# TensorE's order within a slot: the second maxima tile goes between the two transposed products of the second head

## The reference

```python
x = x + _L0_attn_a_ref(_layernorm(x, axis=-1), ...)   # causal mask
x = x + _L0_ffn_ref(_layernorm(x, axis=-1), ...)      # tokens split into two classes
x = x + _L0_attn_b_ref(_layernorm(x, axis=-1), ...)   # rotary, no mask
x = x + _L0_ffn_ref(_layernorm(x, axis=-1), ...)      # classes again
```

## Time and profile before

| | us |
|---|---|
| median of 3 runs (lowest, highest) | 5199.68 (5198.17, 5214.73) |
| the profiled execution | 5192.83 |
| its span, first to last instruction | 5191.0 |
| PE busy, DVE busy, ACT busy in the span | 4514.9, 3178.9, 2550.6 |
| CAUSAL stage, 0 to 1485 us: PE busy, DVE busy | 1234.4, 716.5 |
| first SPLIT stage, 1485 to 2830 us | 1176.6, 883.1 |
| ROTARY stage, 2830 to 4125 us | 1143.8, 810.1 |
| last SPLIT stage, 4125 to 5191 us | 960.1, 769.2 |

### The profile page before, as it was taken

The page is one execution under the profiler, slowest core; times in us unless marked ns, Lnnn a source line. Parts: engine busy times, 40 slices in busy tenths (PEclk is TensorE's granted clock), DMA queues, the critical chain, the costliest instruction groups (busy, mean ns, idle before and its releaser), DMA issues. The chain is left out here.

```text
span 5191.0 us, 90278 instructions
## 1 busy us (share of the span) xinstructions
PE 4514.9 (87%) x26116; PEld 1909.3 (37%) x26116; DVE 3178.9 (61%) x6578; ACT 2550.6 (49%) x3362; POOL 1655.2 (32%) x922
## 2 busy tenths in 40 slices
PE   4988988899869999899995999999989599889889
PEld 2444444445413333333332333333333233333333
DVE  3545545455447667676663766666666277777776
ACT  1444444444435554455551655555555265555555
POOL 2354544545422434434434133332333300000000
PEclk8999999999979999999997999999999799999999
DMA  4343434344223334233232223323323322222221
GB/s 148 97 149 125 143 119 145 123 135 135 94 67 104 95 92 120 81 110 107 94 109 81 83 87 116 114 87 104 114 89 103 83 75 84 80 79 80 75 75 51
DMA packets 302300, 525.68 MB, mean 101 GB/s; under 512 B 58340, under 2 KB 236136, under 8 KB 285544
## 3 DMA queue, kind: packets, MB, share of 16 engines
q1 hardware_dynamic: 259432, 485.06, 31.5%
q10 hardware_dynamic: 42496, 35.66, 2.1%
HBM read 316.97 MB, written 201.46 MB: 100 GB/s over the span
## 5 line engine op out<-in xcount | busy, mean ns | idle before, releaser
L923 DVE TENSOR_REDUCE neg_max<-scores 128x1 f32<-128x512 f32 (+3 forms) x4096 | 2490.0, 636 | 1448.8 <-PE scores L1282 856.2
L1141 ACT ACTIVATE probs<-scores_t 128x1024 f32<-128x1024 f32 (+2 forms) x2048 | 1926.3, 947 | 1683.0 <-PE scores_t L1315 1193.9
L1282 PE MATMUL scores<-k_stack,q_stack 98*128 98x512 bf16 (+4 forms) x4096 | 1454.2, 378 | 311.0 <-DVE neg_max L923 216.5
L1315 PE MATMUL scores_t<-q_stack,k_stack 100*128 100x512 bf16 (+3 forms) x4096 | 1211.5, 370 | 130.6 <-DMA q_stack<-shift_rows 72.7
L1336 PE MATMUL o_ps<-probs,values 128*32 128x512 f32 (+1 forms) x8192 | 1039.7, 580 | 0.9 <-issue 0.6
L1282 PEld LDWEIGHTS scores<-k_stack,q_stack 96*128 96x128 bf16 (+1 forms) x4096 | 400.3, 98 | 1721.8 <-DVE neg_max L923 1243.9
L1315 PEld LDWEIGHTS scores_t<-q_stack,k_stack 100*128 100x128 bf16 x4096 | 382.3, 100 | 467.5 <-issue 292.1
L766 POOL TENSOR_TENSOR parts<-qk_f,parts 128x1024 bf16<-128x1024 f32 x128 | 272.3, 2128 | 707.8 <-ACT parts L1184 527.4
L779 POOL TENSOR_TENSOR x_res<-x_res,o_bias_s 128x1024 f32<-128x1024 f32 x32 | 75.6, 2364 | 1054.7 <-DMA x_res<-x_after 1054.7
L786 POOL TENSOR_TENSOR sim_inv<-sim_parts,minus_half 128x64 f32<-128x64 f32 x32 | 337.6, 10550 | 196.1 <-DVE sim_parts L1006 196.1
L737 POOL TENSOR_SCALAR var_eps<-mean_var 128x4 f32<-128x4 f32 x64 | 14.6, 229 | 1082.6 <-DVE mean_var L887 1082.6
(11 more groups left out here) (118 smaller groups left out, 4015.8 us busy)
## 6 DMA issues: line engine op xcount, KB each, us to landing
q_stack<-q_parts SPq DMA_DIRECT2D x1536, 64.0 KB, 2.5
values<-v_stage SPq DMA_DIRECT2D x64, 1024.0 KB, 4.2
values<-values SPq DMA_DIRECT2D x64, 1024.0 KB, 5.4
k_parts<-parts SPq DMA_DIRECT2D x192, 256.0 KB, 2.5
q_parts<-parts SPq DMA_DIRECT2D x192, 256.0 KB, 4.1
k_stack<-k_parts SPq DMA_DIRECT2D x256, 192.0 KB, 3.0
k_stack<-k_parts SPq DMA_DIRECT2D x256, 128.0 KB, 3.1
x_after<-x_res ACTq DMA_DIRECT2D x48, 512.0 KB, 2.9
```

What stands on the lines that cost most here:

```text
L923: nc.vector.tensor_reduce(neg_max[:, h % G, t:t + 1], bank[:, 0:n], AX.X, ALU.max, negate=True).then_inc(max_done.sem, 1)
L1141: nc.scalar.activation(probs[c][:, h % G, 0:n], st[i][:, 0:n], ACT.Exp).then_inc(exp_done.sem, 1)
L1282: last = nc.tensor.matmul(bank[:, 0:n], q[0:r, h, t * P:(t + 1) * P], k[0:r, h, 0:n], start=True, stop=kind != CAUSAL)
L1315: last = nc.tensor.matmul(st[i][:, off:off + L - q0], k[0:ROWS, h, kt * P:(kt + 1) * P], q[0:ROWS, h, q0:L], start=True, stop=kind != CAUSAL)
```

## The change

`scores_t` gets the list of key tiles that it is to compute, and it tells ScalarE (`st_full`) only with the second tile of the pair. The body now calls it three times: once for A0 and A1, once for B0 and once for B1. PE's order in a slot becomes A0 A1, m0, the first turn, B0, m1, B1, m2, V, m3, the second turn.

```diff
-            def scores_t(B, h, c, i):
+            def scores_t(B, h, c, i, kts):
...
-                for kt in (2 * c, 2 * c + 1):
+                for kt in kts:
...
-                last.then_inc(st_full.sem, 1)
+                if 2 * c + 1 in kts:
+                    last.then_inc(st_full.sem, 1)
...
-                    scores_t(B, h0, c, 0)
+                    scores_t(B, h0, c, 0, (2 * c, 2 * c + 1))
                     max_tile(0)
+                    turns(0)
+                    scores_t(B, h1, c, 1, (2 * c,))
                     max_tile(1)
-                    turns(0)
-                    scores_t(B, h1, c, 1)
+                    scores_t(B, h1, c, 1, (2 * c + 1,))
                     max_tile(2)
```

## The result

| kernel | median us | runs | from | to | profiled execution | its span |
|---|---|---|---|---|---|---|
| before | 5198.93 | 4 | 5182.39 | 5214.73 | 5192.83 | 5191.0 |
| changed | 5280.34 | 4 | 5257.29 | 5290.36 | 5287.39 | 5285.6 |

The ratio of the changed kernel to the one before is 1.0161, with a 95% interval of 1.0132 to 1.0190. Forecast was plus 51 us; it is plus 81. The direction held, and the size did not: 5280.34 lies just above the 5225 to 5280 us that the prediction thought most likely, and 2 us inside the end of its range of 5207 to 5282.

A forecast was written before the change was run, and what follows sets the result against it. PE (busy 87%) waits for DVE's reductions of maxima tiles, and turns wait for their one bank. Losses less gains, 3.49 us per batch times 14.5, add 51 us to 5192.8: 5244, or 5251 for the median; range 5207 to 5282.

The forecast's parts named there:

- Slots without a first turn: nothing: In slots without a first turn, m1's wait comes back at m2: 0.00 to 0.01 us in nearly all, stages 2 to 4.
- the spacing pays: Rival: m1's wait goes and doesn't reappear at m2, so faster, 5120 to 5190 us; chance 0.08.
- both cancel: Rival: the turn's release follows PE more, halving the losses, so no change, 5216 us or less; chance 0.12.
- The turn already waits: ROTARY slot 12 and slot 6: the turn starts no sooner and the whole m1 is lost, 0.22 to 0.23 us.
- The turn just doesn't wait: ROTARY slot 10 and similar SPLIT slots: the turn, coming sooner, now waits for its bank; a loss of 0.20 us.
- The turn behind a shift: Slots 3 and 11, behind `shift_rows`: turn 0.10 us sooner, m1 0.22 more, a loss of 0.12 us.
- In slots 7 it drowns: In slots 7, the 0.12 us loss of a turn behind a shift disappears in DVE's wait.
- The gains: Where m1 waits and the turn doesn't: 0.38 us in slot 9 of two stages, 0.30 in first SPLIT 14 and ROTARY 4.
- What is won back: Where the second turn waits for the first, m1 covers that: 0.18 us in CAUSAL slot 1, 0.14 in 12, 0.09 in slots 13.
- CAUSAL slot 5: The later m1 delays `v_stage` on DVE and so the turn `out`: 0.24 us on top of 0.18, 0.42 lost.
- The sum per batch: Net loss over the four stages: 1.51, 0.63, 0.60 and 0.75, together 3.49 us per batch.
- more is queued on DVE: Rival: later m1s push DVE's turns in the `og` slots too, 12 us more per stage, 5290 us; chance 0.12.

The follow-up runs named there:

- the kernel that has nothing else: The kernel before with NEW only in slots 0 to 3 of the first batch of each stage; 5198.15 us, ratio 1.0028.
- NEW: The changed kernel's order against the kernel before: first turn, B0, m1, B1; in all slots 5280.34 us, ratio 1.0161.
- OLD: The order of the kernel before: m1, first turn, B0 B1; in all slots 5198.93 us.
- the one that changes nothing else: The kernel before with NEW only in slot 15 of both SPLIT stages; 5200.13 us, ratio 1.0016.

## Why the direction was right and the size wrong

Of the 94.6 us between the two profiled spans, the slot periods of batches 1 to 14 are 58.8, slots 0 to 3 at the starts of stages 6.5 (3.4, 2.7 and 0.4; 9.3 in the kernel that has nothing else), the loop's head 8.6, the other slots of batches 0 and 15 6.6. That makes 80.5. That the medians differ by as much (81) can be chance, since these parts come from one pair of profiles. The remaining 14 us are differences that don't repeat from batch to batch, the largest in slots 7 of the first two stages (4.8 and 5.4 us); I didn't trace them one by one, and they are of the order of what single runs of one kernel scatter.

The step that failed is the term "Slots without a first turn: nothing". It was forecast at 0 us, and NEW in those slots alone costs 0.38%, some 20 us, of a forecast that fell short by 30. The slots with a first turn alone cost 1.38%, more than the forecast's 51 us too, by mis-sized slots (10 us) and by the head of the loop (8.6 us), which no term had. The two halves add up to 1.0176, somewhat more than the 1.0161 of the whole, so the shares are good to some 10 us only. Point by point:

- **Plain slots, inside the stages: right.** m1 0.51 and m2 1.17 us after m0, as the arithmetic had it. The rival "the spacing pays" falls with that, and "both cancel" falls with slot 12, where the turn starts no sooner than before.
- **Plain slots as a whole: the step that failed.** "Slots without a first turn: nothing" was worked out at the full clock, with a batch in full course, for stages 2 to 4, and the CAUSAL stage's plain slots had no term. At the low clock m1's lateness does reach m3 (9.3 us in three stage starts); in the CAUSAL stage it reaches DVE's work ahead of slot 9 (0.20 us per batch, 3 us in all). Some 8 us of the 20 stay open.
- **The head of the loop: missing.** Slot 15 has a first turn, so this belongs to the turn slots: the prediction gave it 0.06 us, and it costs 0.17, and 8.6 us more over twelve loop heads of the SPLIT stages.
- **The turn already waits: right.** The turn starts 0.91 us after m0, m2 3.38 against 3.39 forecast. The whole m1 is lost. Slot 6 was forecast at 0.31, with 0.08 for DVE; it is 0.22, and 0.04 in slot 7.
- **The turn just doesn't wait: right** but for 0.02: slot 10 lost 0.22, forecast 0.20.
- **The turn behind a shift: mis-sized.** 0.12 was forecast, 0.17 measured. The prediction moved the turn as a block; its first weight load ran under m1 and now stands open. "In slots 7 it drowns" holds in the first SPLIT stage and ROTARY (+0.04), not in the last SPLIT stage (+0.21); that fewer turns leave DVE free there is a guess. Slot 15 there costs 0.17, not 0.06.
- **The gains: right** (0.37 and 0.30, forecast 0.38, 0.30 and 0.24), and one was missed: ROTARY slot 15 is 0.21 shorter. CAUSAL slot 15 scatters from -0.95 to +0.68, with no gain over the batches.
- **What is won back: wrong in slots 13.** The 0.09 that m1 between the two turns was to give back doesn't come: ROTARY slot 13 lost 0.22, forecast 0.14, CAUSAL slot 13 0.17, forecast 0.10. ROTARY slot 14 lost 0.20, forecast 0.10. In CAUSAL slots 1 and 12 all came back (forecast all but 0.04).
- **CAUSAL slot 5: right** (0.38, forecast 0.42).
- **The sum per batch** is 4.20 us instead of 3.49: 1.76, 0.81, 0.56, 1.06 by stage against 1.51, 0.63, 0.60, 0.75. That explains 10 of the 30 missing us, and it is so little in part by luck: slot 6, forecast 0.09 too high in three stages, makes up for others that were too low. The clock at the starts and the loop's head, which no term of the sum had, explain 15 to 18.
- **The range** went up to 5282 with "more is queued on DVE" as the only way to be slower still. Its mechanism fell (slot 6), and the costs that came were in no rival, so that the measured time lies inside the range by luck. Two of its sums don't come out either: 0.08 us in half of ten turns is 0.4 us per batch, 6 us in one stage and 23 in four, not 15; and 12 us per stage in four stages on top of 5251 is 5299, not 5290.

## What to carry to other kernels

An operation that covers another's wait has to stay in front of it, or something else as long has to take its place: here the tile m1 stands best, in most slots with a turn, between the two products of the next head with the turn behind them, which covers m1's wait, the turn's and m2's at once. When a slot's arithmetic gives zero, do it again for the stretches in which the engine is at its low clock, for the last slot of a loop and for whoever comes behind on the other engines. Those places are few, but here they were a fifth to a quarter of the loss. And where slots differ in what they wait for, an order for each kind of slot is worth more than one for all.

## What the hardware showed that I had not expected

- After the pause between stages PE got its full clock 3.4 to 7.5 us after the first product in one order, and 12.6 to 16.7 us in 16 of 18 places in others, which have a pause of 0.14 or 0.56 us in a slot, though the profile counts PE as busy for 4.00 of 4.00 us in two of the low stretches. It costs 3 us each time.
- The stall at the head of a loop grew from 3.96 to 4.47 us in one SPLIT stage, and from 17.4 to 23.9 us over six loops in the other, with NEW instead of OLD in the slot ahead of it (the first pair of numbers from the changed kernel, the second from the one that changes nothing else). A packet of the instruction queue starts 2.6 to 3.5 us before PE goes on.
- A turn of four transposes takes 0.44 us when its first weight load runs under the product before it, and 0.50 when it has to wait for its bank first.
